# Self attention's rows of maxima at the 5th step, packs ahead of values, and a self projection without rotated weights

## The chip, the cores and the metric

The kernel runs on one core of a Trainium2 chip. The core has TensorE (PE) for matrix products, VectorE (DVE), ScalarE (ACT), GpSimd (POOL) and SyncE (SP), which here only issues DMAs. Each engine works through its own queue of instructions in order and waits on semaphores for the others. The metric is the device time of one execution in microseconds; the median of the runs counts.

## The reference

One cross attention block and one decoder block over 8 batches of 512 tokens with 256 channels. What matters here, cut:

```python
q = (layernorm(x) @ Wq.T + bq); k = ctx @ Wk.T + bk; v = ctx @ Wv.T + bv     # 16 heads of 16, 1601 context rows
x = x + softmax(q k / 4) v @ Wo.T + bo
x0 = layernorm(x)
r = rmsnorm(x0) * g1
q, k, v = r @ wq, r @ wk, r @ wv
q = q * cos + rotate_half(q) * sin          # rotate_half: (-second half, first half) of a head's 16 dims
k = k * cos + rotate_half(k) * sin
h = x0 + softmax(causal(q k / 4)) v @ wo
out = x + h + moe(rmsnorm(h))               # 8 experts, top 2
```

## The kernel before

The program is a row of stages with a barrier between them: `prepare_weights`, `project_inputs`, `attention` (cross), `invert_denominators`, `project_self`, `attention` (self, causal), `finish_self`, `route`, `experts`. The change touches the first, `project_self` and both attentions.

**project_self** handles one batch of 512 tokens per turn. The helper `turns` writes, for each engine, one list of steps with a lag each: in turn t the step of lag d works on batch t - d. The list is the order of the engine's queue. Steps of one batch, in the order in which the data goes: `load` (SP), `divide` (DVE, attention output times the inverse denominators), `out_product` (PE), `residual` (DVE: `x1`, and mean and variance), `deviation` (ACT), `layer_norm` (DVE: `h0`, then a second pass of statistics over `h0`), `root_mean_square` (ACT), `rms_inverse` (DVE), `scale_rows` (ACT: `xr`), `turn_rows` (PE transpose), `take_turned` (ACT: `xT`), `q_products`, `v_product`, `k_products` (PE), `take_v` (ACT). For w = 0 (q) and w = 1 (k) there follow `rope` (DVE: cosine and sine products out of PSUM), the POOL addition to `full`, `high` (ACT: the bf16 part), `subtract_high` (DVE), `middle` (ACT), the POOL subtraction for the low part, and the stores. Nearly every tile is there once, so that each step also waits until the reader of the batch before is through. The rotated half comes from a second product with rotated weights (`wq_rot`, `wk_rot`) into `ps_b`, beside the plain one in `ps_a`; these two tiles are shared by q and k.

**attention** works on 32 units (a batch and 4 heads). In the self attention a unit has 16 steps: step s computes transposed scores `ps_st` (PE, `scores`), ACT takes the exponential into `probs`, and PE multiplies a group of 4 steps with the values into `ps_o` (`products`). The maxima of a row must be known beforehand: 16 "pieces" per unit compute plain scores `ps_s` on PE, and DVE reduces each to a maximum. POOL splits the 16 columns of maxima into three bf16 parts (`split`), PE transposes them ("turn", L659), ACT copies them to `nm_rows` (`copy_max`, L812), and a DMA on ACT's queue (`send_max`, L817) puts them as three more rows into the q pack, where the score product subtracts them. A unit's first `scores` waits for that DMA (`m_rows_in`). Where the pieces of later units stand between the steps is set by `TAIL`: piece k stands at step 16 - TAIL + k - 16, counted from the start of its own unit, so negative values lie in the unit ahead or the one ahead of that. With 11, unit u holds pieces 11 to 15 of unit u+1 at steps 0 to 4, the turn at step 8, and pieces 0 to 10 of unit u+2 at steps 5 to 15. SP loads four buffers of packs (`load_kq`, 12 DMAs for a unit, three units ahead) and of values (`load_v`, 4 DMAs).

## Time and profile before

| what | us |
|---|---|
| median of three runs | 3004.8 |
| lowest and highest | 2999.98, 3007.11 |
| the profiled execution, its own time | 2997.89 |
| span of its trace | 2995.7 |
| cross attention (285 to 1590 in the trace) | 1305 |
| self projection (first load 1599 to first instruction of the self attention 1824) | 225 |
| self attention (1824 to 2215) | 391 |
| experts (2390 to the end) | 606 |

Over the span PE is busy 90%, DVE 60%, ACT 48% and POOL 20%. The views give for a group of instructions the busy time, the mean of one and the idle time of the engine ahead of it with the one that ended it; the view in order of time gives the start, the length and, in brackets, that idle time.

### The profile page before, as it was taken

Reading aid. Unit: us, or ns where it says so; the run is one execution under the profiler, and the core shown is the slowest. Engines: PE = TensorE matmul, PEld = TensorE weight load, DVE = VectorE, ACT = ScalarE, POOL = GpSimd, SP = SyncE. Lnnn points to the kernel's source line nnn. Section 1 sums busy time; section 2 is a strip of 40 time slices with the busy share of each in tenths; the row PEclk is TensorE's granted clock in tenths of the full one; section 3 lists DMA queues with packets and bytes.
Section 4 is the critical chain, followed back from the end, with each engine's and each line's share of the span. In section 5 each row is a group of like instructions: output and inputs, shape, how many; then the busy total and the mean of one; then the engine's idle time right before and its main releaser. Section 6 shows DMA issues by size and latency. Waiting matters only on the chain. (4 is left out here: it accounts for less than half of the span.)

```text
span 2995.7 us, 58252 instructions
## 1 busy us (share of the span) xinstructions
PE 2682.0 (90%) x14814; PEld 1362.6 (45%) x14815; DVE 1802.7 (60%) x3882; ACT 1440.4 (48%) x2927; POOL 588.1 (20%) x815
## 2 busy tenths in 40 slices
PE   7996899999999999999995995888878499999996
PEld 4664233233323333333322552444436377777775
DVE  4654888787878787878853764666634522222221
ACT  2332277676767676767772332656532022222221
POOL 2444200000000000000001543111114433333332
PEclk9998699999999999999997997999988799999998
DMA  6776855453545555545304645677747212212113
GB/s 202 226 215 178 85 63 63 56 65 50 64 51 63 64 63 64 63 54 63 51 14 122 194 161 111 134 142 130 139 114 218 86 30 32 33 32 33 32 32 75
DMA packets 494474, 274.83 MB, mean 92 GB/s; under 512 B 309248, under 2 KB 462736, under 8 KB 494064
## 3 DMA queue, kind: packets, MB, share of 16 engines
q1 hardware_dynamic: 472176, 239.83, 41.9%
q0 software_dynamic: 16192, 30.16, 5.2%
q10 hardware_dynamic: 5888, 2.24, 0.4%
q8 instruction: 99, 1.62, 0.3%
q14 instruction: 119, 0.97, 0.2%
HBM read 172.22 MB, written 103.31 MB: 92 GB/s over the span
## 5 line engine op out<-in xcount | busy, mean ns | idle before, releaser
L731 DVE TENSOR_REDUCE att_cross_neg_max<-att_cross_ps_s 128x1 f32<-128x401 f32 x2048 | 1030.8, 567 | 225.4 <-PE att_cross_ps_s L650 223.0
L806 ACT ACTIVATE att_cross_probs<-att_cross_ps_st 128x512 f32<-128x512 f32 (+1 forms) x1664 | 882.6, 601 | 345.3 <-PE att_cross_ps_st L669 327.3
L650 PE MATMUL att_cross_ps_s<-att_cross_k_pack,att_cross_q_pack 96*128 96x401 bf16 x2048 | 666.0, 348 | 29.7 <-DMA att_cross_q_pack<-q_parts 29.2
L669 PE MATMUL att_cross_ps_st<-att_cross_q_pack,att_cross_k_pack 99*128 99x512 bf16 (+1 forms) x1664 | 641.9, 389 | 37.0 <-issue 30.8
L684 PE MATMUL att_cross_ps_o<-att_cross_probs,att_cross_v_tiles 128*32 128x512 f32 (+1 forms) x3328 | 452.1, 616 | 0.1
L650 PEld LDWEIGHTS att_cross_ps_s<-att_cross_k_pack,att_cross_q_pack 96*128 96x128 bf16 x2048 | 203.1, 99 | 402.7 <-DVE att_cross_neg_max L731 233.9
L669 PEld LDWEIGHTS att_cross_ps_st<-att_cross_q_pack,att_cross_k_pack 99*128 99x128 bf16 (+1 forms) x1664 | 165.5, 100 | 341.4 <-ACT att_cross_probs L806 192.5
L731 DVE TENSOR_REDUCE att_self_neg_max<-att_self_ps_s 128x1 f32<-128x128 f32 (+3 forms) x512 | 224.1, 485 | 158.3 <-PE att_self_ps_s L653 154.3
L806 ACT ACTIVATE att_self_probs<-att_self_ps_st 128x256 f32<-128x256 f32 (+3 forms) x512 | 205.9, 441 | 145.4 <-PE att_self_ps_st L672 136.0
L777 POOL CAST att_cross_neg_max_parts<-att_cross_neg_max_merged 128x16 bf16<-128x16 f32 x32 | 6.3, 196 | 1193.3 <-DVE att_cross_neg_max_merged L724 1193.3
L1857 DVE COPY moe_hiddenT<-moe_ps_h 128x256 f32<-128x256 f32 x142 | 60.2, 424 | 297.0 <-PE moe_ps_h L1760 297.0
L1814 ACT ACTIVATE moe_silu<-moe_ps_g 128x352 f32<-128x352 f32 x142 | 65.7, 463 | 300.9 <-PE moe_ps_u L1752 300.9
L669 PE MATMUL att_self_ps_st<-att_self_q_pack,att_self_k_pack 99*128 99x256 bf16 (+3 forms) x512 | 158.5, 312 | 46.6 <-DMA att_self_q_pack<-att_self_neg_max_rows 42.3
L1770 PE MATMUL moe_ps_y<-top_wd_sb,moe_hiddenT 128*128 (+1 forms) x852 | 196.0, 379 | 1.1 <-DVE moe_hiddenT L1858 1.1
L1752 PE MATMUL moe_ps_g<-top_wg_sb,moe_rowsT 128*128 x568 | 192.8, 462 | 0.0
L1752 PE MATMUL moe_ps_u<-top_wu_sb,moe_rowsT 128*128 x568 | 192.0, 461 | 0.0
L650 PE MATMUL att_self_ps_s<-att_self_k_pack,att_self_q_pack 96*128 96x128 bf16 (+3 forms) x512 | 158.5, 314 | 28.5 <-DMA att_self_q_pack<-q_parts 28.3
L1770 PEld LDWEIGHTS moe_ps_y<-top_wd_sb,moe_hiddenT 128*128 128x128 f32 (+1 forms) x852 | 161.7, 190 | 35.1 <-issue 1.4
L1712 POOL DMA_INDIRECT sums<-moe_y,moe_target x71 | 113.5, 1598 | 280.4 <-ACT moe_y L1820 136.1
L1851 DVE TENSOR_TENSOR moe_hidden<-moe_ps_u,moe_silu 128x352 f32<-128x352 f32 x142 | 73.4, 517 | 132.9 <-ACT moe_silu L1814 132.9
L684 PEld LDWEIGHTS att_cross_ps_o<-att_cross_probs,att_cross_v_tiles 128*32 128x32 f32 (+1 forms) x3328 | 66.5, 109 | 154.0 <-ACT att_cross_probs L806 129.2
L1752 PEld LDWEIGHTS moe_ps_u<-top_wu_sb,moe_rowsT 128*128 128x128 f32 x568 | 108.5, 191 | 60.7 <-issue 1.0
(225 smaller groups left out, 3045.3 us busy)
## 6 DMA issues: line engine op xcount, KB each, us to landing
att_cross_k_pack<-k_parts SPq DMA_DIRECT2D x192, 200.1 KB, 6.7
k_parts<-in_part SPq DMA_DIRECT2D x72, 256.0 KB, 3.1
in_rows<-in_ctx_dram SPq DMA_DIRECT2D x24, 512.0 KB, 4.4
v_rows<-in_v_biased SPq DMA_DIRECT2D x24, 512.0 KB, 3.0
att_cross_q_pack<-q_parts SPq DMA_DIRECT2D x192, 64.0 KB, 7.7
att_cross_v_tiles<-v_rows SPq DMA_DIRECT2D x128, 96.0 KB
att_self_k_pack<-k_parts SPq DMA_DIRECT2D x192, 64.0 KB, 3.6
att_self_q_pack<-q_parts SPq DMA_DIRECT2D x192, 64.0 KB, 3.7
```

Of the source, the lines that this page charges most:

```text
L650: mm = nc.tensor.matmul(ps_s[bank][:, 0:w], qp[v.buf][0:SROWS, j, q * P:(q + 1) * P], kp[v.buf][0:SROWS, j, s:s + w], start=True, stop=not ...
L669: mm = nc.tensor.matmul(ps_st[bank_of_step[s]][0:rows, q0:SEQ], kp[u.buf][0:MROWS, j, t * P:t * P + rows], qp[u.buf][0:MROWS, j, q0:SEQ], ...
L684: nc.tensor.matmul(ps_o[j * VW:(j + 1) * VW, q0:SEQ], va[u.vbuf][0:rows, t, j, :], pr[0:rows, (u.odd * STEPS + t * GH + j) % RING, q0:SEQ] ...
L731: nc.vector.tensor_reduce(nmax[v.odd][:, j * QT + q, i:i + 1], ps_s[bank][:, 0:w], AX.X, ALU.max, negate=True).then_inc(s_read, 1)
L777: link(nc.gpsimd.tensor_copy(nm_parts[:, 0, :], full))
L806: nc.scalar.activation(pr[0:rows, (u.odd * STEPS + s) % RING, q0:SEQ], ps_st[bank_of_step[s]][0:rows, q0:SEQ], ACT.Exp).then_inc(exp_done, 1)
L1712: pool.indirect_dma_start(out=sums, in_=y[t.par][:, :], in_offset=None, compute_op=ALU.add, out_offset=bass.IndirectOffsetOnAxis(ap=target ...
L1752: last = nc.tensor.matmul(ps[half][:, 0:HHALF], xT[t.par][:, i, :], wt[:, bass.ds(at, HHALF)], start=(i == 0), stop=(i == KC - 1))
L1770: last = nc.tensor.matmul(ps_y[:, :], hT[half][0:CW[c], c, :], wd[0:CW[c], bass.ds(at, DIM)], start=(half == 0 and c == 0), stop=(half == ...
L1814: nc.scalar.activation(sil[half][:, :], ps_g[half][:, 0:HHALF], ACT.Silu).then_inc(sil_ready, 1)
L1851: nc.vector.tensor_tensor(h[half][:, :], ps_u[half][:, 0:HHALF], sil[half][:, :], ALU.mult)\
L1857: nc.vector.tensor_copy(hT[half][:, 0:CH - 1, :], ps_h[half][:, 0:CH - 1, :])
```

## The change

1. **Channels of q and k by dim, not by head.** `WqT`, `WkT`, `wq`, `wk`, `bq`, `bk` are permuted in `prepare_weights` so that channel d*16 + h holds dim d of head h. A half of every head then lies in one of the two blocks of 128 partitions, and the rotated half is the other block. The packs of both attentions are read from the new layout; the DMAs keep their number and their rows (16x4x1601 and 16x4x512), only the address from which each row comes is another: the four rows of one partition are now neighbours in memory.
2. **No rotated weights.** `rope_products` computes one product per q and k, into a PSUM tile of its own for each (`ps_qk`). `rope` reads both blocks of it.
3. **Layer norm on ACT, no second statistics.** The mean square of `h0` follows from the variance (variance times the square of 1/std). `xr` is made straight from `x1` by one scale and one bias per row; `h0` too, later and on ACT.
4. **Other turns in `project_self`:** the lags go up to 5, and POOL's addition and low part are steps of their own.
5. **Self attention:** `TAIL` is 15, and SP issues the packs ahead of the values.

```diff
-                nc.scalar.mul(d[:, :, 0, :], s[:, :, 1, :], -1.0)
-                last = nc.scalar.copy(d[:, :, 1, :], s[:, :, 0, :])
+                for n in ("wq", "wk"):
+                    last = nc.scalar.copy(keep[n][:, :, :].rearrange("p c (d h) -> p c d h", d=HD),
+                                          raw[n][:, :, :].rearrange("p c (h d) -> p c d h", d=HD))
...
-    TAIL = 11 if causal else 15
+    TAIL = 15
...
-                                     k_parts[v.batch, K_PARTS[r], v.rows, :].rearrange("(j d) n -> d j n", d=HD))\
+                                     k_parts[v.batch, K_PARTS[r], :, :].rearrange("(d h) n -> d h n", d=HD)[:, v.heads, :],
...
+                    if not causal:
+                        next_values(u, after, before)
                     if after >= 3:
...
                         load_kq(u.next(3))
+                    if causal:
+                        next_values(u, after, before)
...
-                    for ps, weights in ((ps_a, ("wq", "wk")[w]), (ps_b, ("wq_rot", "wk_rot")[w])):
+                    for o in range(KC):
+                        for i in range(KC):
+                            last = nc.tensor.matmul(ps_qk[w][:, o, :], keep[("wq", "wk")[w]][:, i, o * P:(o + 1) * P],
+                                                    xT[:, i, :], start=(i == 0), stop=(i == KC - 1))
...
-                turns(pe, batches, ((1, turn_rows), (0, out_product), (1, q_products), (1, v_product),
-                                    (1, k_products)))
+                turns(pe, batches, ((3, turn_rows), (2, out_product), (3, q_products), (3, v_product),
+                                    (3, k_products)))
...
+                def mean_square(b):
                     dve.wait_ge(std_ready, b + 1)
                     nc.vector.reciprocal(norm.rstd[:, :], norm.std[:, :])
                     dve.drain()
+                    nc.vector.tensor_tensor(norm.square[:, :], norm.rstd[:, :], norm.rstd[:, :], ALU.mult)
+                    minus(minus_mean[0], norm.rstd)
                     dve.drain()
+                    nc.vector.tensor_tensor(norm.ms[:, :], norm.square[:, :], norm.mv[:, :, 1], ALU.mult)\
+                      .then_inc(ms_ready, 1)
...
+                    nc.vector.scalar_tensor_tensor(out=t2[w][:, 0, :], in0=ps_qk[w][:, 1, :], scalar=-1.0,
+                                                   in1=keep["sin_" + "qk"[w]][:, :], op0=ALU.mult, op1=ALU.mult)
+                    last = nc.vector.tensor_tensor(t2[w][:, 1, :], ps_qk[w][:, 0, :], keep["sin_" + "qk"[w]][:, :],
+                                                   ALU.mult)
...
-                turns(act, batches, ((1, take_turned), (2, lambda b: high(1, b)), (0, deviation),
-                                     (2, lambda b: middle(1, b)), (1, take_v), (1, lambda b: high(0, b)),
-                                     (0, root_mean_square), (0, scale_rows), (1, lambda b: middle(0, b))))
+                turns(act, batches, ((4, lambda b: high(0, b)), (3, take_turned), (4, lambda b: middle(0, b)),
+                                     (4, lambda b: high(1, b)), (2, deviation), (2, root_mean_square),
+                                     (2, scale_rows), (4, lambda b: middle(1, b)), (3, take_v), (2, layer_norm)))
...
-                turns(pool, batches, ((3, lambda b: add_and_split(1, b)), (0, add_bias),
-                                      (2, lambda b: add_and_split(0, b))))
+                turns(pool, batches, ((4, lambda b: add_rotated(1, b)), (4, lambda b: low(0, b)), (1, add_bias),
+                                      (4, lambda b: low(1, b)), (3, lambda b: add_rotated(0, b))))
```

How the change moves instructions, at three places. First DVE in the loop of `project_self`, one turn, as it stands before from the residual on (`slf_x` is `x1`, `slf_h` is `h0`, `slf_roped` is `full`, `slf_roped_rest` what is left after the high part):

```order
L1050 TENSOR_TENSOR slf_x<-slf_ps_o,slf_x_biased 128x1024
L187 BN_STATS slf_norm_stats<-slf_x 128x6 x4
L190 BN_AGGR slf_norm_mean_var<-slf_norm_stats 128x2 x4
L1043 REGISTER_ALU
L1044 TENSOR_TENSOR slf_o_normed<-slf_oT,slf_inv_rows 128x1024
```

The rotary products of q follow (four rows), and then:

```order
L1056 RECIPROCAL slf_norm_std_inv<-slf_norm_std 128x4
L1060 TENSOR_SCALAR slf_h<-slf_x,slf_norm_mean_var,slf_norm_std_inv 128x256 x4
L187 BN_STATS slf_norm_stats<-slf_h 128x6 x4
L190 BN_AGGR slf_norm_mean_var<-slf_norm_stats 128x2 x4
L200 TENSOR_TENSOR slf_norm_mean<-slf_norm_mean_var 128x4
L202 TENSOR_TENSOR slf_norm_mean_square<-slf_norm_mean,slf_norm_mean_var 128x4
L1068 RECIPROCAL slf_norm_rms_inv<-slf_norm_rms 128x4
```

And now, in the same loop, from the division on:

```order
L1064 TENSOR_TENSOR slf_o_normed<-slf_oT,slf_inv_rows 128x1024
L1082 RECIPROCAL slf_norm_std_inv<-slf_norm_std 128x4
L1084 TENSOR_TENSOR slf_norm_mean<-slf_norm_std_inv 128x4
L1077 SCALAR_TENSOR_TENSOR slf_norm_minus_mean<-slf_norm_mean_var,slf_norm_std_inv 128x4
L1087 TENSOR_TENSOR slf_norm_mean_square<-slf_norm_mean,slf_norm_mean_var 128x4
L1092 RECIPROCAL slf_norm_rms_inv<-slf_norm_rms 128x4
L1094 TENSOR_TENSOR slf_norm_scale<-slf_norm_std_inv,slf_norm_rms_inv 128x4
L1077 SCALAR_TENSOR_TENSOR slf_norm_minus_mean<-slf_norm_mean_var,slf_norm_scale 128x4
L1113 TENSOR_TENSOR slf_roped_rest<-slf_roped,slf_roped_part 128x1024
```

The large operation on `slf_h` and its statistics are gone from DVE; seven operations of 4 columns stand between the division and the subtraction for k.

Second, ACT in the self attention, from the exponential of step 8 (256 wide) on, before:

```order
L806 ACTIVATE att_self_probs<-att_self_ps_st 128x256
L810 ISA
L811 ISA
L812 COPY att_self_neg_max_rows<-att_self_ps_s 48x128
L804 REGISTER_ALU
L806 ACTIVATE att_self_probs<-att_self_ps_st 128x256
L817 DMA att_self_q_pack<-att_self_neg_max_rows 3x16x128
```

Now, from the exponential of step 4 (384 wide) on:

```order
L818 ACTIVATE att_self_probs<-att_self_ps_st 128x384
L822 ISA
L823 ISA
L824 COPY att_self_neg_max_rows<-att_self_ps_s 48x128
L833 REGISTER_ALU
L835 COPY att_self_out_buf<-att_self_ps_o 128x512
L816 REGISTER_ALU
L817 REGISTER_ALU
L818 ACTIVATE att_self_probs<-att_self_ps_st 128x384
L829 DMA att_self_q_pack<-att_self_neg_max_rows 3x16x128
```

The copy and the DMA of the maxima stand four steps earlier and now enclose the copy of the finished output.

Third, SP in the self attention, where a unit's values and packs meet, before:

```order
L594 ISA
L594 DMA att_self_v_tiles<-v_rows 128x4x16
L583 ISA
L583 DMA att_self_k_pack<-k_parts 16x4x512
L586 DMA att_self_q_pack<-q_parts 16x4x512
```

Now:

```order
L589 DMA att_self_k_pack<-k_parts 16x4x512
L592 DMA att_self_q_pack<-q_parts 16x4x512
L600 ISA
L600 DMA att_self_v_tiles<-v_rows 128x4x16
L600 ISA
```

The 12 DMAs of the packs are issued first, the 4 of the values behind them.

## Rows read from the trace of the kernel before

**Rows 1.** Windows: busy time by engine, clock, DMA share, GB/s; self projection
```profile
core 0: us, PE busy (x) PEld busy (x) DVE busy (x) ACT busy (x) POOL busy (x), PEclk, DMA share, GB/s
...
1615.00:1805.00 190.00, 170.40 (x556) 101.24 (x557) 127.08 (x282) 65.76 (x102) 86.95 (x57) 0.96 0.56 175
```
**Rows 2.** In order of time: start, length, engine, line; PE, one turn
```profile
1673.18 1.09 PE L1006 MATMUL slf_ps_t<-top_keep_constants,slf_x_rms 128*128 128x128 f32 x8 [1.24 <-ACT slf_x_rms L1107]
...
1677.56 3.60 PE L1015 MATMUL slf_ps_a<-slf_xT,top_keep_wq 128*128 128x512 f32 x8
...
1680.99 3.60 PE L1015 MATMUL slf_ps_b<-slf_xT,top_keep_wq_rot 128*128 128x512 f32 x8
...
1696.15 1.09 PE L1006 MATMUL slf_ps_t<-top_keep_constants,slf_x_rms 128*128 128x128 f32 x8 [1.24 <-ACT slf_x_rms L1107]
```
**Rows 3.** In order of time: the steps of the new ring, from three turns
```profile
1623.31 0.16 DVE L202 TENSOR_TENSOR slf_norm_mean_square<-slf_norm_mean,slf_norm_mean_var 128x4 f32<-128x4 f32 x1 [0.42 <-issue]
...
1623.84 0.18 DVE L1068 RECIPROCAL slf_norm_rms_inv<-slf_norm_rms 128x4 f32<-128x4 f32 x1 [0.36 <-ACT slf_norm_rms L1101]
...
1671.34 1.71 ACT L1107 ACTIVATE slf_x_rms<-slf_h,slf_norm_rms_inv 128x256 f32<-128x256 f32 x4 [0.24 <-DVE slf_norm_rms_inv L1068]
...
1672.95 1.03 ACT L1129 CAST slf_roped_part<-slf_roped_rest 128x1024 bf16<-128x1024 f32 x1
...
1676.15 2.35 POOL L1150 TENSOR_TENSOR slf_roped<-slf_rope_cos,slf_rope_sin 128x1024 f32<-128x1024 f32 x1
...
1678.61 1.04 ACT L1125 CAST slf_roped_part<-slf_roped 128x1024 bf16<-128x1024 f32 x1 [3.04 <-POOL slf_roped L1150]
...
1680.83 1.22 DVE L1050 TENSOR_TENSOR slf_x<-slf_ps_o,slf_x_biased 128x1024 f32<-128x1024 f32 x1
...
1683.92 1.19 DVE L1044 TENSOR_TENSOR slf_o_normed<-slf_oT,slf_inv_rows 128x1024 f32<-128x1024 f32 x1
```
**Rows 4.** Instructions of a tile: shortest/median/longest ns; and one division in order of time
```profile
L1060 DVE TENSOR_SCALAR slf_h<-slf_x,slf_norm_mean_var,slf_norm_std_inv x32: 401/811/2410, 1618.4 to 1782.2; 128x256 f32<-128x256 f32 x32
L187 DVE BATCH_NORM_STATS2 slf_norm_stats<-slf_h x32: 408/409/428, 1620.8 to 1783.7; 128x6 f32<-128x256 f32 x32
...
L1144 POOL TENSOR_TENSOR slf_x_biased<-slf_x_rows,top_keep_bo x32: 714/769/1711, 1607.1 to 1758.5; 128x256 f32<-128x256 f32 x32
...
1635.55 1.45 DVE L1044 TENSOR_TENSOR slf_o_normed<-slf_oT,slf_inv_rows 128x1024 f32<-128x1024 f32 x1
```
**Rows 5.** In order of time: first transpose of the stage; first instruction of the next stage
```profile
1625.89 1.97 PE L1006 MATMUL slf_ps_t<-top_keep_constants,slf_x_rms 128*128 128x128 f32 x8 [12.12 <-ACT slf_x_rms L1107]
...
1824.13 7.03 POOL L751 MEMSET att_self_k_pack<- 3x2048 bf16 x4 [6.32 <-POOLq L66]
```
**Rows 6.** Who waited for whom, self attention, PE: us in total, times, longest
```profile
PE att_self_ps_st L669 <- DMA att_self_q_pack<-att_self_neg_max_rows: 42.3, 28, 2.4
...
PE att_self_ps_s L650 <- DMA att_self_q_pack<-q_parts: 2.5, 6, 1.1
```
**Rows 7.** Windows, columns as in rows 1: two units of the self attention
```profile
1953.46:1965.09 11.63, 9.67 (x97) 5.16 (x98) 6.93 (x16) 6.86 (x18) 1.37 (x5) 1.00 0.74 136
...
2066.50:2079.40 12.90, 11.24 (x98) 5.81 (x99) 7.07 (x16) 7.12 (x18) 1.37 (x5) 0.87 0.67 121
```
**Rows 8.** In order of time: ACT in the unit that starts at 1953.46
```profile
1956.32 0.49 ACT L806 ACTIVATE att_self_probs<-att_self_ps_st 128x384 f32<-128x384 f32 x1 [0.17 <-PE att_self_ps_st L672]
1956.70 0.58 ACT L823 COPY att_self_out_buf<-att_self_ps_o 128x512 f32<-128x512 f32 x1
...
1958.97 0.38 ACT L806 ACTIVATE att_self_probs<-att_self_ps_st 128x256 f32<-128x256 f32 x1 [0.52 <-PE att_self_ps_st L672]
...
1959.52 0.73 ACTq L817 DMA_DIRECT2D att_self_q_pack<-att_self_neg_max_rows  x1
```
**Rows 9.** First pack DMA of that unit on SP; issues: KB, us to landing
```profile
1958.42 0.37 SPq L583 DMA_DIRECT2D att_self_k_pack<-k_parts  x1
...
att_self_k_pack<-k_parts SPq DMA_DIRECT2D x192, 64.0 KB, 3.6
```
**Rows 10.** In order of time: a load of single elements on ACT's queue, first stage
```profile
1.38 0.48 ACTq L96 DMA_DIRECT2D top_keep_bk<-in_bk_dram  x1
```

136 lines of the change are left out of this document (78 added, 58 removed).

## Prediction

> **What bounds the kernel now.** I read the windows by stage first, then the order of time of one turn and one unit, then who waited for whom. Two stages change in substance; the cross attention keeps its steps, and only the addresses of its packs are other ones, so I cost it at nothing: its packs are loaded three units ahead of their use.
>
> In the self projection PE is the bound. One turn, from one transpose of a batch to the next, takes 1696.15 - 1673.18 = 22.97 us, and only 1.24 us of it PE waits, for `scale_rows` on ACT [rows 2]. Over the stage PE is busy 170.4 of 190 us, DVE 127.1, POOL 87.0 and ACT 65.8, with the DMA engines at 0.56 [rows 1].
>
> In the self attention PE has 9.67 us of work in a unit of 11.63 us [rows 7]; the rest is one wait at the unit's start, for the DMA that brings the rows of maxima: 42.3 us over the stage, besides 2.5 us for packs at the maxima's products [rows 6]. A unit can also run at a lower granted clock: 0.87 instead of 1.00 of the 2.4 GHz level, with 11.24 us of PE work instead of 9.67 [rows 7].
>
> **The self projection, term by term.**
>
> *PE.* The eight products with a rotated weight take 1680.99 - 1677.56 = 3.43 us [rows 2], and there are two such blocks in a turn: 6.86 us go. PE is left with 22.97 - 1.24 - 6.86 = 14.9 us. That is the least a turn can take, if nothing else becomes longer.
>
> *What is late next.* The new lists of turns close a ring of single buffers, over which exactly one turn passes: `high` of q (ACT, first in its turn) waits for POOL's addition of q, which stands last in POOL's turn, behind the low part of k; that waits for `middle` of k on ACT, which stands behind `scale_rows`; that waits for both scales on DVE, which stand behind mean square, division and residual; and the residual stands behind the subtraction for q, which waits for `high` of q. From start to start, with rows of before: `high`, subtraction, up to the residual 1680.83 - 1678.61 = 2.22; residual with moments up to the division 1683.92 - 1680.83 = 3.09; division 1.19; reciprocal and three small operations up to the mean square, about 0.6 at 0.16 to 0.18 each with their drains; mean square, root on ACT, up to the reciprocal 1623.84 - 1623.31 = 0.53; reciprocal, scale and minus mean, up to ACT, about 0.7; `scale_rows` up to `middle` 1672.95 - 1671.34 = 1.61; `middle` and low part up to the addition 1676.15 - 1672.95 = 3.20; the addition up to `high` 1678.61 - 1676.15 = 2.46. The sum is 15.6 us [rows 3]. It is above PE's 14.9, so the ring sets the turn, not PE; PE would show about 0.7 us or more of idle time in each.
>
> *Collisions on DVE and POOL.* The same `tensor_scalar` takes 401 ns at its shortest and 2410 at its longest, about one POOL addition more; one of POOL's bias additions takes 1711 instead of 769 ns, and a division that starts among them 1.45 instead of 1.19 us [rows 3, 4]. In the ring the subtraction for q starts 1.1 us after `high`, while POOL does the addition of k, which always follows that of q. Its price lies between 0 and what the addition has left, 2.46 - 1.1 - 0.1 = 1.2 us. The nearest rows say that operations do lose time to each other, the division only part of it, so I take 0.9: a turn of **16.5 us**. The operation that suffers most in before, `tensor_scalar` on `h0`, is gone from DVE.
>
> *Unseen operations.* A `scalar_tensor_tensor` on 128x512 out of PSUM has no row; I take it to cost what the plain product does that it replaces, or up to half as much again; it is not in the ring. ACT's `layer_norm` costs what `scale_rows` does, 1.71 us [rows 3], at the end of ACT's turn: ACT's work becomes 65.8 / 8 + 1.7 = 9.9 us of 16.5, hidden. POOL keeps its 87 / 8 = 11 us [rows 1], hidden but for the ring's part.
>
> *DMA.* The stage moves the same bytes. Its share of 0.56 [rows 1] is 0.56 x 22.97 = 12.9 us of all engines per turn; with turns of 16.5 us it would be 0.78. The loads of a batch are asked for about a turn ahead of their use, so I hide them; below 13 us DMA would be the bound.
>
> *Sum.* Seven turns between the eight transposes: 7 x (22.97 - 16.5) = 45.3 us. Ahead of the first transpose, `h0` with four operations and the second statistics leave the chain: by the shortest and the median row 4 x 0.40 to 4 x 0.81, and 4 x 0.41 [rows 4], 3.2 to 4.9 us, less 0.5 for the added small operations. I take 3.7. Behind the last transpose, 1824.13 - 1625.89 - 7 x 22.97 = 37.4 us pass up to the next stage [rows 5]. Of them 6.9 us of products go, but the transpose now stands some 4 us ahead of its `take_turned`, since that waits behind `high` of q: I count 3 us. Together **52 us**, with 46 for turns of 17.4 and 63 for 14.9.
>
> **The self attention.** The DMA of the maxima is issued 6.06 us after the unit's start and the next unit begins 5.57 us after the issue [rows 7, 8]. Four steps earlier it stands behind the exponential of step 4, which starts 2.86 us in [rows 8]; with the 0.55 us from exponential to issue seen at step 8, 0.58 for the output copy that now comes between, and 0.1 for the wider exponential it is issued at about 4.1 us and lands at about 9.7. PE is through with its work at 9.7. So nearly all of the 42.3 us goes [rows 6].
>
> What comes back: ACT now has both copies and the issue (0.58 and 0.73 us for the latter two [rows 8]) between steps 4 and 6, where the exponentials are long. From step 8 on PE would wait for banks of scores by about 0.2 us a unit: 6 us. Late landings I put at 2 us. For the packs: pieces of the unit after next begin at step 1 instead of 5, some 3 us earlier in a unit that is 1.5 us shorter. Before, their first DMA is issued 4.96 us into a unit [rows 7, 9], after the values; now they can start when the unit does. Issued 12 times at 0.48 us [rows 10] and landed 3.6 us later [rows 9] they are there 9.4 us in, and needed at about 9.9 + 0.5 us. So the other 2.5 us go as well [rows 6]. The values are loaded three units ahead and have slack. The four more pieces ahead of unit 0 lie under its own maxima DMA, some 5 us. Clock: units at 0.87 cost 1.6 us more [rows 7]; without the idle gap fewer may occur. Between 0 and 11 us I take 5, three such units. Sum: 42.3 + 2.5 - 6 - 2 + 5 = **42 us**.
>
> **The first stage.** Two more DMAs of single elements on ACT's queue, 0.48 us each [rows 10], ahead of the load that ACT waits for: 1 us lost. Copying two weights permuted replaces four half copies.
>
> **Total.** 52 + 42 - 1 = 93 us. The profiled execution took 2997.9 us: 2904.9. The median of the runs is 6.9 us higher, 3004.8, which gives **2912 us**.
>
> **A rule on the shared port.** The division and the subtractions read two SBUF tiles on DVE, and POOL reads SBUF all along [rows 3]. The Trainium skill, "SBUF — State Buffer", section "SBUF: two separate sides", says that such a DVE operation and a POOL operation exclude each other for a whole instruction: whoever starts first keeps the port, the other blocks fully. By that rule, the longest `tensor_scalar` fits, while the division's 1.45 us [rows 4] shows a shorter block.
>
> **Rivals.**
> *Full blocking.* The subtraction for q loses the whole 1.2 us and the division up to one bias addition, 0.7 us: turns of 15.6 + 1.9 = 17.5 us, 7 us more, 2919. For it: the 2410 ns. Against: the division's row. 0.15.
> *Nothing in the way.* PE sets the turn at 14.9, and the clock stays up in all units: 63 + 48 - 1 = 110 us, 2895. Against it: the ring's sum. 0.12.
> *Late rows of maxima.* They are now issued while SP issues the tail of the packs and then the values, whose rows are 64 bytes (16 numbers). If landing grows from 5.6 to 7 us, a unit takes 11.1: 0.5 us instead of 1.4 are won, 16 us, and the total is 67: 2938. 0.10.
> *Slower: packets at another price.* A unit's packets fill all DMA engines for 0.74 x 11.63 = 8.6 us [rows 7]. The packs are most of them and are now read from neighbouring rows. Should such packets cost more, DMA sets the unit from a factor of 9.9 / 8.6 = 1.15 on, and against the 11.63 us of that unit the whole change loses from 13.3 us a unit, a factor of 1.54. At 1.6 it is 13.8 us: 31 x (13.8 - 11.63) = 67 us lost, 51 won, 3021. Row length and count are unchanged, so 0.03.
>
> **How the numbers follow.** Forecast 0.60. The range takes in the faster rival and the late rows: from turns of 14.9 and full clock (2895, less some run to run spread of 7) to turns of 18 with half of the attention's gain (61 us, 2944): 2888 to 2946. Only the slower rival lies on the other side; 0.2% (6 us) is about what can be told from no change: faster 0.96, same 0.01, slower 0.03.
>
> **What would show it.** Transposes in the self projection 16.5 us apart, PE idle in between for ACT (`take_turned` behind `high`), the subtraction for q longer than 1.22 us or late; the stage about 173 us from its first load to the next one's first instruction. In the self attention: the wait for the rows of maxima under 5 us in total, unit starts 9.9 to 10.1 us apart, waits of `ps_st` for ACT's exponentials grown. Wrong: a turn under 15 or over 17.5 us; waits on `q_parts` at step 1; a cross attention that changes by more than 5 us.

## The result, and the profile of the changed kernel

| | before | after |
|---|---|---|
| median, us | 3002.39 (4 runs, 2995.71 to 3007.11) | 2912.36 (4 runs, 2911.49 to 2918.69) |
| the profiled execution, us | 2997.89 | 2918.69 |

The ratio is 0.9706 with an interval of 0.9682 to 0.9731: 90 us less by the medians, where 2912 us was forecast. The profiled execution of after is the slowest of its four runs, and that of before one of the faster ones, so the two traces differ by less, 79 us. Of all executions reported here one stood apart: one of the four of the kernel with `TAIL` alone took 4596.66 us at a mean granted clock of 0.551, where its other three had 0.932 or 0.933, and it is left out of every figure.

**The self projection.** In order of time, the changed kernel: the first load of the stage, its first and last transpose, and the first instruction of the next stage (they answer to [rows 5]; the load of before stands at 1598.68).

```profile
1600.03 0.70 SPq L896 DMA_DIRECT2D slf_oT<-out_rows  x1
...
1624.66 1.96 PE L1026 MATMUL slf_ps_t<-top_keep_constants,slf_x_rms 128*128 128x128 f32 x8 [9.24 <-ACT slf_x_rms L1139]
...
1746.65 1.06 PE L1026 MATMUL slf_ps_t<-top_keep_constants,slf_x_rms 128*128 128x128 f32 x8
...
1784.53 7.03 POOL L763 MEMSET att_self_k_pack<- 3x2048 bf16 x4 [6.37 <-POOLq L66]
```

The stage takes 184.5 us instead of 225.45, 41 us less. The seven turns take 1746.65 - 1624.66 = 122.0 us; before they took 161.5, from the transpose at 1625.89 to the last one at 1787.36. Four take 18.1 to 18.23 each, the three nearest the ends 16.2 to 16.6. The first transpose comes 24.6 us after the load instead of 27.2, and what follows the last one takes 37.9 instead of 1824.13 - 1787.36 = 36.8.

One turn and two units of the self attention in windows (columns as in [rows 1]):

```profile
1675.66:1693.88 18.22, 15.13 (x56) 9.78 (x56) 14.59 (x28) 10.69 (x18) 12.60 (x9) 1.00 0.85 256
...
1884.00:1904.00 20.00, 19.65 (x196) 10.30 (x195) 13.85 (x32) 14.02 (x37) 2.75 (x10) 1.00 0.76 154
```

PE is busy 15.13 of the 18.22 us, so it is no longer the bound of a turn. In order of time, PE in that turn (it answers to [rows 2]):

```profile
1675.66 1.09 PE L1026 MATMUL slf_ps_t<-top_keep_constants,slf_x_rms 128*128 128x128 f32 x8 [1.62 <-ACT slf_v_rows L1159]
...
1681.68 3.70 PE L1034 MATMUL slf_ps_qk<-slf_xT,top_keep_wq 128*128 128x512 f32 x8 [1.47 <-ACT slf_xT L1153]
```

PE waits twice for ACT, and ACT waits in turn. This is the ring (the closed chain of waits over several engines that one turn has to pass), once around, in order of time (it answers to [rows 3]; the row of POOL at 1685.86, the four bias additions, stands beside it):

```profile
1676.87 4.65 POOL L1190 TENSOR_TENSOR slf_roped<-slf_rope_cos,slf_rope_sin 128x1024 f32<-128x1024 f32 x2
...
1679.34 1.04 ACT L1165 CAST slf_roped_part<-slf_roped 128x1024 bf16<-128x1024 f32 x1 [1.75 <-POOL slf_roped L1190]
...
1680.41 2.20 DVE L1113 TENSOR_TENSOR slf_roped_rest<-slf_roped,slf_roped_part 128x1024 f32<-128x1024 f32 x1 [2.81 <-ACT slf_roped_part L1165]
1682.53 1.21 DVE L1072 TENSOR_TENSOR slf_x<-slf_ps_o,slf_x_biased 128x1024 f32<-128x1024 f32 x1
...
1685.61 1.37 DVE L1064 TENSOR_TENSOR slf_o_normed<-slf_oT,slf_inv_rows 128x1024 f32<-128x1024 f32 x1
1685.86 3.75 POOL L1184 TENSOR_TENSOR slf_x_biased<-slf_x_rows,top_keep_bo 128x256 f32<-128x256 f32 x4
1686.90 0.16 DVE L1082 RECIPROCAL slf_norm_std_inv<-slf_norm_std 128x4 f32<-128x4 f32 x1
1687.14 0.44 DVE L1084 TENSOR_TENSOR slf_norm_mean<-slf_norm_std_inv 128x4 f32<-128x4 f32 x1
...
1687.73 0.54 DVE L1087 TENSOR_TENSOR slf_norm_mean_square<-slf_norm_mean,slf_norm_mean_var 128x4 f32<-128x4 f32 x1
1688.64 0.18 DVE L1092 RECIPROCAL slf_norm_rms_inv<-slf_norm_rms 128x4 f32<-128x4 f32 x1 [0.36 <-ACT slf_norm_rms L1133]
1688.89 0.74 DVE L1094 TENSOR_TENSOR slf_norm_scale<-slf_norm_std_inv,slf_norm_rms_inv 128x4 f32<-128x4 f32 x1
...
1689.91 2.08 ACT L1139 ACTIVATE slf_x_rms<-slf_x,slf_norm_minus_mean,slf_norm_scale 128x256 f32<-128x256 f32 x4 [1.30 <-DVE slf_norm_minus_mean L1077]
1691.89 1.03 ACT L1169 CAST slf_roped_part<-slf_roped_rest 128x1024 bf16<-128x1024 f32 x1
...
1693.00 2.14 POOL L1195 TENSOR_TENSOR slf_roped_part<-slf_roped_rest,slf_roped_part 128x1024 bf16<-128x1024 f32 x1 [3.38 <-ACT slf_roped_part L1169]
1695.10 4.66 POOL L1190 TENSOR_TENSOR slf_roped<-slf_rope_cos,slf_rope_sin 128x1024 f32<-128x1024 f32 x2
...
1697.57 1.05 ACT L1165 CAST slf_roped_part<-slf_roped 128x1024 bf16<-128x1024 f32 x1 [1.75 <-POOL slf_roped L1190]
```

From `high` of q to `high` of q are 1697.57 - 1679.34 = 18.23 us, the length of a turn. The row of POOL at 1676.87 holds two additions, of q and then of k; the second ends at 1681.52. The subtraction for q, started at 1680.41, ends 1.1 us after that: it stood still for as long as the addition ran, and then took its time.

**The self attention.** Who waited for whom, PE, over the stage (it answers to [rows 6]):

```profile
PE att_self_ps_s L671 <- POOL att_self_neg_max_parts L793: 6.8, 29, 1.4
...
PE att_self_ps_st L681 <- ACT att_self_probs L818: 0.8, 3, 0.3
PE att_self_ps_st L681 <- DMA att_self_q_pack<-att_self_neg_max_rows: 0.4, 1, 0.4
```

The 42.3 us of waits for the rows of maxima are 0.4. A new, small one stands in nearly every unit: PE is at the turn of the maxima 0.2 us before POOL has split them. Units start 10.0 us apart. From the start of the first unit to that of the last are 2119.40 - 1808.57 = 310.8 us instead of 2202.34 - 1847.87 = 354.5, 43.6 us less. PE was busy for 309.15 us of that stretch before, at a mean granted clock of 0.97, and is for 303.24 us now, at 0.99: 37.7 us of the gain are idle time, 5.9 are shorter busy time. ACT in the unit that starts at 1890.87 (it answers to [rows 8]):

```profile
1894.12 0.26 ACT L824 COPY att_self_neg_max_rows<-att_self_ps_s 48x128 bf16<-48x128 bf16 x1
...
1894.71 0.74 ACTq L829 DMA_DIRECT2D att_self_q_pack<-att_self_neg_max_rows  x1
```

The DMA is issued 3.84 us into the unit instead of 6.06.

**The rest.** The first load of rows for the next stage is issued 1.7 us later than before, 0.85 in a second profile of the same kernel; ahead of it stand the added loads of single elements of `bq` and `bk` on ACT's queue. The cross attention takes the same, to 1 us. The products of the finish stage span 2.3 us more in this profile; in the second profile they do not, so that is scatter.

### The profile page after: what moved, and what is told of

It reads as the page before. It is cut to its first block and busy times, and to the rows that moved or that the text cites. A ratio compares the mean times of both kernels' runs of the same rounds, so it can differ in the third digit from the quotient of the medians.

```text
span 2916.9 us, 57933 instructions
## 1 busy us (share of the span) xinstructions
PE 2630.9 (90%) x14686; PEld 1338.9 (46%) x14687; DVE 1780.8 (61%) x3810; ACT 1461.8 (50%) x2957; POOL 593.5 (20%) x815
## 3 DMA queue, kind: packets, MB, share of 16 engines
q1 hardware_dynamic: 472176, 239.83, 42.6%
q8 instruction: 100, 1.64, 0.3%
## 5 line engine op out<-in xcount | busy, mean ns | idle before, releaser
(222 smaller groups left out, 2971.5 us busy)
```

## The experiments

Two questions are open. Is it the 5th step (`TAIL`) that took the 42 us of waits, as the prediction had it? And does the ring hold the turn of the self projection, and what does it consist of? The kernel before, run beside all kernels up to `proj_only` but `late_packs`, had a median of 3005.92 us.

**The self attention's part alone.** The kernel before with change 5 alone.

```diff
-    TAIL = 11 if causal else 15
+    TAIL = 15
...
+                    if causal:
+                        next_values(u, after, before)
```

> The kernel before with change 5 alone (TAIL 15 and packs ahead of values in the self attention; the projections as they were). My theory (the unit was held by the landing of its rows of maxima, and both edits together remove that): 42 to 44 us under the kernel before, unit starts 10.0 us apart, the wait for the rows of maxima under 1 us in total. Rival (part of what the self attention gained comes from the new layout of the packs, with neighbouring rows in memory): clearly less, units of 10.5 us or more.

Measured: 2953.24 us (2952.76 to 2954.83), 52.7 us under before, a ratio of 0.983 (0.9805 to 0.9856). Units stand 10.0 us apart, and no wait for the rows of maxima is listed; from the first unit's start to the last's are 311.4 us. The profiles differ by 45 us; the medians by more, since the kernel before scatters from 2995.6 to 3012.0. So the gain does not need the new layout. With packs first and `TAIL` 11 the two layouts can be compared too: 308.0 us from the first unit's start to the last's in the old one (att_order), 308.5 in the new one (rope_tail11).

**TAIL alone.** Packs stay behind the values.

> The kernel before with TAIL 15 alone, values still issued ahead of the packs. With pieces of the unit after next from step 1 on, the packs are needed about 10.5 us into the unit that loads them. My theory: issued behind 4 value DMAs the first pack is issued at about 5 us, the twelfth at about 10.5, landed at about 14: a unit takes at least 13.5 us, so PE waits for q_parts at step 1 and the kernel is about 60 us slower than before. Rival (the order of SP does not matter, since the packs have slack): as att_both, some 43 us under before, no waits for q_parts.

Measured: 3048.41 us (three runs, 3046.96 to 3049.09), a ratio of 1.0143 (1.0109 to 1.0177): 42.5 us slower than before, where I expected about 60. Who waited for whom, and one unit in order of time:

```profile
PE att_self_ps_s L650 <- DMA att_self_q_pack<-q_parts: 90.0, 31, 25.4
```

```profile
1949.02 0.47 SPq L583 DMA_DIRECT2D att_self_k_pack<-k_parts  x1
...
1954.37 0.38 SPq L586 DMA_DIRECT2D att_self_q_pack<-q_parts  x1
...
1957.32 0.28 PE L650 MATMUL att_self_ps_s<-att_self_k_pack,att_self_q_pack 96*128 96x128 bf16 x1 [2.33 <-DMA att_self_q_pack<-q_parts]
```

The last pack is issued at 1954.37 and PE goes on at 1957.32, when it has landed. Units take 13.6 us and more, as expected (13.5 at least). The waits for the rows of maxima are gone, and a longer one stands in their place.

**The order of SP alone.** TAIL stays 11.

```diff
-                def unit(u, after, before=True):
+                def next_values(u, after, before):
...
+                    if causal:
+                        next_values(u, after, before)
```

> The kernel before with the packs ahead of the values in the self attention alone, TAIL still 11. My theory: only the waits for q_parts (2.5 us in total) go, and the unit stays held by the rows of maxima: 0 to 2.5 us under before, which may not be told from none. Rival (the order is what gives the gain, because the DMA of the maxima lands sooner when it collides with other packets): over 10 us under before, the wait for the rows of maxima well below 42 us.

Measured: 2951.39 us (2950.92 to 2952.76), a ratio of 0.9822 (0.9796 to 0.9847): **54.5 us under before**, where I expected at most 2.5. The rival won. The rows of maxima are still copied and sent at the 9th step, and yet the wait for them falls from 42.3 to 7.6 us:

```profile
PE att_self_ps_st L675 <- DMA att_self_q_pack<-att_self_neg_max_rows: 7.6, 17, 1.4
```

From two units of this kernel in order of time, issues on ACT and on SP and one unit start on PE:

```profile
1944.54 0.73 ACTq L823 DMA_DIRECT2D att_self_q_pack<-att_self_neg_max_rows  x1
```

```profile
1943.62 2.08 SPq L594 DMA_DIRECT2D att_self_v_tiles<-v_rows  x4
...
1947.52 0.33 SPq L583 DMA_DIRECT2D att_self_k_pack<-k_parts  x1
...
1952.70 0.38 SPq L586 DMA_DIRECT2D att_self_q_pack<-q_parts  x1
```

```profile
1948.38 0.39 PE L675 MATMUL att_self_ps_st<-att_self_q_pack,att_self_k_pack 99*128 99x512 bf16 x1 [0.24 <-DMA att_self_q_pack<-att_self_neg_max_rows]
```

From the issue at 1944.54 to the start that waited for its landing are 3.84 us; in before they are 5.57 [rows 7, 8]. In before the 12 packs are issued from 4.96 us into a unit on [rows 9], so that the DMA of the maxima, at 6.06, falls among them. Here they are all issued by 1953.1, 1.4 us before the next DMA of the maxima at 1954.45. What the DMA of the maxima falls among here are the four loads of values (32 KB each, 1943.62 to 1945.7), and among them it lands early, which points to the packs; `late_packs` below tests it. In before, the units whose start waited for this DMA start 4.5 to 6.0 us after its issue, here 3.8 to 4.2 but for the first, 5.0. The start of the last unit, with no packs and no values being loaded any more, comes 3.3 us after the issue in before and 3.4 here. The DMA view over 1850 to 2200 us has the same 12 KB DMAs as a queue of their own (packets, MB, share of the 16 engines' time); before, then this kernel:

```profile
q10 hardware_dynamic: 1530, 0.37, 1.0%
```

```profile
q10 hardware_dynamic: 1581, 0.38, 0.5%
```

About the same packets took twice the time where they are issued among the packs. In att_both they are issued among them again, with 1.1% of the time, but early enough for nobody to wait.

The clock has a share in the gain. From the first unit's start to the last's this kernel takes 308.0 us, 46.4 less than before. PE was busy for 299.62 us of it at a mean granted clock of 0.99, before for 309.15 at 0.97, with the same products: 36.9 us are idle time gone, 9.5 are the same work done faster.

**Packs first, but late.** Is it the collision, or did the values in front delay the maxima? att_order with one more wait.

```diff
-                            sp.wait_ge(st_done, u.n * STEPS + RING)
+                            sp.wait_ge(st_done, u.n * STEPS + (8 if causal else 0) + RING)
```

> The kernel before with packs ahead of values in the self attention (as att_order), but the packs also wait for the scores of step 7, so that SP issues them some 4.2 us into a unit, about where the kernel before issues them (4.96 us); the values follow. Collision theory (in the kernel before the rows of maxima land late because their DMA is issued, 6.06 us into a unit, in the middle of the 12 pack DMAs, and shares the DMA engines with them): the wait for the rows of maxima comes back, 25 to 45 us in total, and the kernel takes about what the kernel before does, at least 2985 us. Rival (the gain of att_order came from the values no longer being in front of the maxima's DMA, wherever the packs stand): the wait stays under 15 us and the kernel within 10 us of att_order's 2951.

Measured: 2992.85 us (10 runs, 2988.51 to 3000.86) beside 3004.86 for before, a ratio of 0.9972 (0.9956 to 0.9988). Some 42 of the 54.5 us are gone again, with no step of ACT or PE moved. Waits, and one unit in order of time, SP and ACT:

```profile
PE att_self_ps_st L675 <- DMA att_self_q_pack<-att_self_neg_max_rows: 35.4, 30, 2.4
```

```profile
1952.84 0.33 SPq L583 DMA_DIRECT2D att_self_k_pack<-k_parts  x1
...
1958.85 0.38 SPq L586 DMA_DIRECT2D att_self_q_pack<-q_parts  x1
```

```profile
1954.74 0.74 ACTq L823 DMA_DIRECT2D att_self_q_pack<-att_self_neg_max_rows  x1
```

The unit after this starts at 1959.52, 4.78 us after the issue. PE's busy time over the units is 309.22 us at a mean granted clock of 0.97 again. The collision theory holds; the values' place is worth at most the 12 us that are left, and the packs also start 0.8 us earlier than in before.

**All but the fifth part.** The changed kernel with TAIL 11 and values ahead of packs.

```diff
-    TAIL = 15
+    TAIL = 11 if causal else 15
...
-                    if causal:
-                        next_values(u, after, before)
```

> The whole change but for its fifth part: TAIL 11 and values ahead of packs in the self attention. My theory (the parts add up): the self projection gives its 41 us, the new layout of the packs gives and takes nothing, so 38 to 41 us under before, and the self attention shows units of 11.6 us and 42 us of waits for the rows of maxima. Rival (the two parts help each other, or the layout changes the packs' price): a gain off by more than 8 us from 41.

Measured: 2965.84 us (2951.55 to 2971.45), 40.1 under before, a ratio of 0.9862 (0.9822 to 0.9902), with 42.6 us of waits for the rows of maxima. 40 and 53 make 93 us; the whole change gave 90 beside one set of runs of before and 95 beside another: the parts add up within the scatter. The units took 365.3 us in this profile, 10.8 more than in that of before, with 315.30 us of busy time at a mean granted clock of 0.95; one profile of each can't tell scatter from a price of the new layout in the old order of SP, and with packs first the layout has none.

For the self projection the next three kernels share a chip with the changed one and with before (3007.25 us).

**The changed kernel again.**

> The changed kernel itself, as the measure for the three beside it. The same times as on record, 2911 to 2919 us, with turns of the self projection 18.2 us apart. It also tells whether the 3 us that finish_self took longer in the one profile of after come again (then the layout or the state of the queues costs them) or not (then they are scatter of single executions).

Measured: 2912.38 us (2908.44 to 2913.89), a ratio of 0.968 (0.9655 to 0.9706), turns of 18.2 to 18.3 us but for the three nearest the ends. The finish stage's products span 67.9 us here, 71.6 in the first profile and 69.3 in before: scatter.

**Products twice.**

```diff
-                    for o in range(KC):
+                    for o in [*range(KC)] * 2:
```

> The changed kernel with each of the products of q and k computed twice into the same tile, so that PE has the same number of products in the self projection as the kernel before. If taking the rotated products away is what made room for the new turns: PE has 6.9 us more work in a turn, 15.1 + 6.9 = 22 us, so the turn is 22 us or more and the kernel about 7 x 3.8 = 26 us slower than the changed one. Rival (the gain came from the new order and the work taken from DVE, PE's products were hidden anyway): less than 10 us slower.

The products of q and k are computed twice into the same place. Measured: 2947.57 us, a ratio of 0.9798 (0.9773 to 0.9824), 35 us slower than the changed kernel, where I expected about 26. One turn in windows:

```profile
1668.60:1690.11 21.51, 21.51 (x73) 12.98 (x72) 13.72 (x27) 10.89 (x17) 13.44 (x8) 1.00 0.72 220
```

PE is busy without a gap, in 21.51 us where I expected 22 or more. The stage takes 215.7 us against 183.3 in the changed kernel run beside it, 32.4 of the 35: its turns near the ends, 16.2 to 17.6 us there, are 21.5 to 23.5 here, which the expectation had not counted. Before, with as much work, a turn took 22.97 us. So the new turns and the smaller DVE work alone are worth some 1.5 us of the 4.75 gained in a turn; the rest needs the products gone.

**POOL's turn exchanged.** The addition of q ahead of the low part of k.

```diff
-                                      (4, lambda b: low(1, b)), (3, lambda b: add_rotated(0, b))))
+                                      (3, lambda b: add_rotated(0, b)), (4, lambda b: low(1, b))))
```

> The changed kernel with the last two steps of POOL's turn exchanged: the addition of q stands ahead of the low part of k. Ring theory (a chain over DVE, ACT and POOL sets the turn of 18.2 us, and POOL's low part of k is a link of it): the addition of q no longer waits for middle of k, so the link scale_rows, middle, low part (about 3 us) leaves the ring; another chain or the products on PE (15 us) are next; I expect a turn of about 16.5 us and 7 x 1.75 = 12 us under the changed kernel. Rival (the turn is set by the share of 0.85 of the DMA engines or by the sum of blocked instructions on DVE): a turn of 18 us or more, no gain.

Measured: 2905.53 us (2902.89 to 2906.67), 6.9 under the changed kernel; the ratio to before is 0.9661 (0.9636 to 0.9686). The ring was cut, but only to 17.55 to 17.64 us a turn instead of some 16.5. The turns together are 4.5 us shorter (118.8 against 123.4); another 3.1 us come behind the last transpose (33.45 against 36.55). One turn in windows, and DVE and POOL in order of time:

```profile
1692.53:1710.17 17.64, 15.11 (x56) 9.80 (x57) 15.48 (x29) 10.81 (x18) 13.66 (x9) 1.00 0.90 271
```

```profile
1695.79 1.98 DVE L1113 TENSOR_TENSOR slf_roped_rest<-slf_roped,slf_roped_part 128x1024 f32<-128x1024 f32 x1 [1.33 <-ACT slf_roped_part L1165]
...
1700.77 2.40 DVE L1064 TENSOR_TENSOR slf_o_normed<-slf_oT,slf_inv_rows 128x1024 f32<-128x1024 f32 x1
```

```profile
1694.56 2.12 POOL L1195 TENSOR_TENSOR slf_roped_part<-slf_roped_rest,slf_roped_part 128x1024 bf16<-128x1024 f32 x1
1696.65 3.34 POOL L1190 TENSOR_TENSOR slf_roped<-slf_rope_cos,slf_rope_sin 128x1024 f32<-128x1024 f32 x1
1699.95 2.13 POOL L1195 TENSOR_TENSOR slf_roped_part<-slf_roped_rest,slf_roped_part 128x1024 bf16<-128x1024 f32 x1
```

DVE is now busy for 15.48 us, and the rest is mostly its wait for POOL's addition and `high`: DVE's own queue is the next ring. Its busy time holds stalls: the division takes 2.40 us, since it starts in POOL's low part of q, which ends at 1702.1, and ends about 1.1 us after it. It goes both ways: the subtraction for q waits for POOL's low part of k, which ends at 1696.7, and the addition of k behind it takes 3.34 instead of 2.35 us, until the subtraction is through.

**POOL's additions in quarters.**

```diff
-                    nc.gpsimd.tensor_tensor(full[w][:, :, :], t1[w][:, :, :], t2[w][:, :, :], ALU.add)\
+                    for c in range(KC):
+                        for s in range(0, SEQ, SEQ // 2):
+                            last = nc.gpsimd.tensor_tensor(full[w][:, c, s:s + SEQ // 2], t1[w][:, c, s:s + SEQ // 2],
+                                                           t2[w][:, c, s:s + SEQ // 2], ALU.add)
```

> The changed kernel with POOL's addition of 128x1024 written as four of 128x256 (in both uses, q and k). Theory of whole blocking (the subtraction for q takes 2.20 instead of 1.22 us because it stands still until the running POOL instruction ends): it now stands still for at most a quarter of the addition, so it takes 1.8 us or less, and the turn is some 0.5 us shorter, less what three more instructions cost POOL: 0 to 5 us under the changed kernel. Rival (both engines share bandwidth by element, whatever the length of the instructions): the subtraction stays at 2.2 us and nothing is gained.

Measured: 2911.84 us (2911.43 to 2912.76), 0.5 under the changed kernel and not to be told from it. In order of time (the row of POOL holds the eight quarters of q and k):

```profile
1690.67 6.51 POOL L1192 TENSOR_TENSOR slf_roped<-slf_rope_cos,slf_rope_sin 128x256 f32<-128x256 f32 x8
```

```profile
1694.65 1.26 DVE L1113 TENSOR_TENSOR slf_roped_rest<-slf_roped,slf_roped_part 128x1024 f32<-128x1024 f32 x1 [1.64 <-ACT slf_roped_part L1165]
```

The subtraction falls from 2.20 to 1.26 us, and the median of all 16 from 1.64 to 1.24, which speaks for whole blocking (a stop until POOL's running instruction ends) and against sharing by element. But the addition of q lies in the ring too: from its start at 1690.67 to `high` at 1693.57 are 2.90 us instead of 2.47, and the subtraction now holds up POOL. Turns in the middle are 17.1 to 18.6 us; what was won was given back.

**The rotary products of q ahead of the subtraction for k**, on top of the exchange on POOL (before beside it: 3004.86 us).

```diff
-                                     (4, lambda b: subtract_high(1, b)), (3, lambda b: rope(0, b))))
+                                     (3, lambda b: rope(0, b)), (4, lambda b: subtract_high(1, b))))
```

> pool_swap with one more exchange, in DVE's turn: the rotary products of q stand ahead of the subtraction for k. In pool_swap the turn took 17.55 us, of which DVE was busy 15.4 and then waited 1.3 us for POOL's addition of q and high of q. Theory (DVE's own queue is the ring there): POOL's addition of q and high of q now run while DVE does the subtraction for k and the rotary products of k (1.14 + 2.4 us), so DVE no longer waits and its busy time or PE's 15.1 us sets the turn: 15.5 to 16.5 us, 7 to 12 us under pool_swap, about 2896. Rival (the DMA engines, at a share of 0.91 in a turn of pool_swap, are the bound by now): a turn of over 17 us, less than 4 us under pool_swap.

Measured: 2912.48 us, a ratio to before of 0.9711 (0.9687 to 0.9735): the gain of the exchange is gone, and turns take 18.5 to 18.9 us. Neither theory named the cause. Who waited for whom (1640 to 1760 us), and ACT and PE in order of time:

```profile
PE slf_ps_t L1026 <- ACT slf_v_rows L1159: 16.2, 6, 3.8
```

```profile
1707.61 1.05 ACT L1169 CAST slf_roped_part<-slf_roped_rest 128x1024 bf16<-128x1024 f32 x1 [1.58 <-DVE slf_roped_rest L1113]
1708.56 1.01 ACT L1159 COPY slf_v_rows<-slf_ps_t 128x1024 f32<-128x1024 f32 x1
```

`middle` of k waits 1.58 us for the subtraction that was moved back, `take_v` stands behind it on ACT, and PE's next transpose needs the tile that `take_v` empties. I had followed DVE and POOL, and not what is queued behind the waiter on ACT.

**take_v ahead of middle of k**, to test that.

```diff
-                                     (2, scale_rows), (4, lambda b: middle(1, b)), (3, take_v), (2, layer_norm)))
+                                     (2, scale_rows), (3, take_v), (4, lambda b: middle(1, b)), (2, layer_norm)))
```

> rope_ahead with one exchange in ACT's turn: take_v stands ahead of middle of k. rope_ahead moved the subtraction for k behind the rotary products of q, so middle of k, and behind it on ACT take_v, came later; PE waited 2.3 to 3.8 us a turn for take_v at its transpose, and the turn took 18.6 us instead of pool_swap's 17.55. If that reading is right, take_v now comes about 1.6 us earlier (it does not wait for the subtraction for k), PE's wait shrinks and the turn is at most 17.5 us: 6 to 10 us under rope_ahead's 2912, near pool_swap's 2905 or below. Rival (the wait for take_v was a symptom; the ring over high, the subtraction for q and the residual holds the turn): still over 18.2 us a turn and within 3 us of rope_ahead.

Measured: **2903.36 us** (2900.82 to 2909.39) beside 3007.58 for before, a ratio of 0.9659 (0.9637 to 0.9681). One turn, and the same wait over the same window:

```profile
1667.36:1684.50 17.14, 15.13 (x56) 9.78 (x56) 14.68 (x28) 10.68 (x17) 14.57 (x9) 1.00 0.90 272
```

```profile
PE slf_ps_t L1026 <- ACT slf_v_rows L1159: 3.6, 5, 1.0
```

Turns take 17.1 to 17.3 us, and PE's wait fell from 16.2 to 3.6 us. The reading holds. With 9 us less than the changed kernel it has the lowest median here, about level with the exchange on POOL alone: its turns are shorter, but the stage as a whole takes 177.1 us against 175.8 there, since the stretch behind the last transpose is 36.45 us again. Its ratio's interval overlaps with that of the changed kernel (0.9655 to 0.9706), which ran on another chip, so that the order of the two is likely rather than settled; the length of the turns, 17.2 against 18.2 us, is plain.

**The 9th step instead of the 5th, all else changed.** rope_ahead with `TAIL = 11 if causal else 15`.

> rope_ahead with TAIL 11 in the self attention, packs still ahead of the values: the rows of maxima at the 9th step as in the kernel before. With the packs first the step of the maxima's DMA should matter little: att_order (TAIL 11) and att_both (TAIL 15) differed by 2 us. Units of 9.85 instead of 10.0 us with some 7 us of waits for the rows of maxima in total: 0 to 4 us under rope_ahead. Rival (my theory of the prediction, by which TAIL 15 is what takes the wait away): 30 us or more over rope_ahead.

Measured: 2911.43 us (2908.93 to 2913.81) beside 2912.48: no difference, with 6.9 us of waits for the rows of maxima. Once the packs stand ahead of the values, the step of the maxima is worth 1 to 2 us at most, and those are for the 9th: att_order is 1.85 us under att_both.

## Why the prediction was right or wrong

The total was right, 2912 forecast and 2912.36 measured, and the mechanism of the self attention was not. Point by point:

**The turn of the self projection: right in kind, 1.7 us too short.** The ring was there, with its links in the order forecast: PE idle for ACT, and 18.23 us from `high` to `high` where 16.5 were forecast. That is beyond the 17.5 us that the prediction itself had named as a sign of being wrong. Of PE's two waits in a turn the forecast had named the one for `take_turned` (1.47 us); the other, 1.62 us at the transpose for `take_v`, which stands behind `middle` of k on ACT, it had not. Link by link, measured against the sum: `high`, subtraction, up to the residual 3.19 (forecast 2.22 + 0.9); up to the division 3.08 (3.09); division 1.29 (1.19); up to the mean square 0.83 (0.6); up to the second reciprocal 0.91 (0.53); up to `scale_rows` 1.27 (0.7); `scale_rows` up to `middle` 1.98 (1.61); up to the addition 3.21 (3.20); the addition up to `high` 2.47 (2.46). The failed step is the one that took the small operations "at 0.16 to 0.18 each". Three of them, all `tensor_tensor`, took 0.44, 0.54 and 0.74 us, since in the new order they stand beside POOL's four bias additions, and each ended, to 0.02 us, with one of these (1687.57, 1688.26, 1689.62): with their waits 1.2 us of the 1.7. In rope_ahead the operation of L1094 started at 1703.51, when the last of these additions was ending (1703.56 to 1703.57), and took 0.16. Another 0.4 is `scale_rows`, which now has a bias per row beside the scale: 2.08 us for four instead of 1.71 [rows 3]. That row was of another form, and I had not bounded the difference.

**The collision of the subtraction: right.** 0.98 us over its 1.22, forecast 0.9 between 0 and 1.2. What was to be hidden stayed hidden: ACT is busy for 10.69 us of a turn (9.9 forecast), POOL for 12.60 (11), and the DMA share is 0.85 (0.78).

**The shared port.** Every subtraction or division that starts while a POOL operation runs ends 1.1 us after that operation, in all turns of before, after, pool_swap, rope_ahead, take_v_ahead and quarters; the only exceptions are two divisions that start within 0.03 us of a bias addition and go first (pool_swap, rope_ahead). It holds in quarters too, where the 1.26 us are 0.18 up to the end of the running quarter (1694.83) and 1.08 behind it. The division of pool_swap took 2.40 and POOL's addition 3.34 us. The Trainium skill, "SBUF — State Buffer", section "SBUF: two separate sides", says that a DVE operation with two inputs in SBUF and a POOL operation that reads SBUF exclude each other for a whole instruction. These rows agree, down to `tensor_tensor` operations of 4 columns. The argument against it, the division's 1.45 us in the kernel before, was wrong: that division starts at 1635.55 in a bias addition that ends at 1635.92, and itself ends at 1637.00, the same 1.1 us behind. It was blocked in full, by what was left of a short operation. The rival of full blocking was nearer with its turn of 17.5 us, but by an addend that did not come: it had up to 0.7 us for the division, which took 1.29 instead of 1.19, and nothing for the small operations.

**Ahead of and behind the turns.** 2.6 us were won ahead of the first transpose (3.8 in the second profile, forecast 3.7), and 1.1 lost behind the last (0.2 won in the second profile, forecast 3 won). By my reading the deeper pipeline takes as long to drain as the products save; no run was made for this, but in pool_swap the stretch was 3.3 us shorter than before. The turns gave 39.5 us instead of 45.3, although most were 1.7 us too long: the three nearest the ends were not, and before the first turn took 24.31 us and not 22.97. Together the stage gave 41 us instead of 52.

**The self attention: size right, cause wrong.** 43.6 us against 42. I took the 5.57 us from issue to next unit for a fixed price, and put the 42.3 us to the step and 2.5 to the order. The order alone gave 54.5 us, the step alone cost 42.5, and with both the order's gain stayed. The landing was late because it fell among the packs (3.84 us in att_order, where it falls among the loads of values); moving the packs took the wait away, and it is also what made TAIL 15 possible, which alone only put a longer wait for the packs in its place. The prediction held the clue in its own rows: packs from 4.96 us, maxima at 6.06. Of the small terms, crowding on ACT (6 us forecast) was 0.8, and 6.8 us of waits for POOL's split, unforeseen, took its place. The waits for packs, 2.5 us in before, are 1.2. For the clock 5 us were forecast: PE's busy time fell by 5.9 us as the mean granted clock rose from 0.97 to 0.99, but some of that are the four pieces that now lie ahead of unit 0. From the eighth unit on, all but the last two took 10.0 us at a granted clock of 1.00.

**First stage and cross attention.** 1.7 us lost where 1 was forecast, 0.85 in the second profile; the cross attention is unchanged.

**The total.** The parts by their own kernels are 40 and 53 us, 93 together, and 93 was the forecast, as 52 + 42 - 1. That 52 was 11 too high and 42 about 10 under what the median of before has to lose: its profiled execution was one of its faster ones. That the waits that went are also what made it scatter is likely, but not shown. Two errors cancelled. With the reasons as they stood, the right total was luck.

## What to carry to other kernels

When a wait for a DMA sets the pace, see first what other DMAs are issued around it, and move those: the time to landing is not a property of the DMA alone. When an instruction is moved later on one engine, follow who waits for it, and then what is queued behind that waiter; twice here (pool_swap, rope_ahead) the link that had not been drawn set the turn. And price small operations beside a busy POOL by the row that stands beside a busy POOL.

## What the runs showed of the hardware that was not expected

- A 12 KB DMA took 3.8 to 4.2 us from issue to the start that waited for it when it was issued among four loads of 32 KB, with the last of twelve of 64 KB issued 1.4 us earlier (att_order); in the middle of the twelve it took 4.5 to 6.0 (before), with no loads around it 3.3, and its packets took twice the engines' time (0.5% against 1.0%).
- `tensor_tensor` operations of DVE of 128x4, with both inputs in SBUF, took 0.44 to 0.74 us beside POOL's bias additions and ended with one of them, and 0.16 without. The reciprocals between them took 0.16 to 0.18 in either place.
- POOL is held up as well: an addition of 2.35 us took 3.34 when a subtraction of DVE had the turn.
- Where the wait for the DMA of the maxima was gone, runs scattered less: 2952.8 to 2954.8 us with the fifth change alone, 2951.6 to 2971.5 with all but it, four runs each.
- The granted clock followed the wait: over the units of the self attention its mean was 0.95 to 0.97 with the wait for the maxima (proj_only, before, late_packs), 0.88 with the longer wait for packs (att_tail), and 0.99 where the wait was gone or small (att_order, att_both, the changed kernel).
